# An attention front without queries: transposed x contracted with the context, keys from the squared key weights

## What is computed

```python
# x: (4, 256, 256), ctx: (4, 256, 64)
kv   = ctx @ W_k.T + b_k                                  # (4, 256, 64)
q    = einsum('bij,bjd->bid', layernorm(x), kv)           # the "queries"
sim  = einsum('bid,bjd->bij', q, kv) * 256 ** -0.5
sim  = (sim - mean(sim)) * rsqrt(var(sim) + 1e-6) * gamma + beta
x    = x + tanh(g_xattn) * softmax(sim)
h    = layernorm(x)
score = sigmoid(h @ gate_weight.T)   # 16 experts in 4 groups; best 2 groups, best 4 experts of them
w    = normalised scores of the picked experts * 2.5, zero elsewhere
out  = x + tanh(g_ffn) * (sum_n w[:, n] * swiglu_n(h) + swiglu_shared(h))
```

## Time and profile before

| | |
|---|---|
| median of 3 launches | 205.99 us (205.96 to 206.59) |
| profiled execution, first to last instruction (its span) | 204.2 us |
| PE busy | 186.4 us, 91% |
| DVE busy | 173.8 us, 85% |
| POOL busy | 95.0 us, 46% |
| ACT busy | 83.5 us, 41% |
| moved by DMA | 18.06 MB |

### The profile page before, as it was taken

The page is one execution under the profiler, slowest core; times in us unless marked ns, Lnnn a source line. Parts: engine busy times, 40 slices in busy tenths (PEclk is TensorE's granted clock), DMA queues, the critical chain, the costliest instruction groups (busy, mean ns, idle before and its releaser), DMA issues.

```text
span 204.2 us, 2910 instructions
## 1 busy us (share of the span) xinstructions
PE 186.4 (91%) x809; PEld 142.1 (70%) x809; DVE 173.8 (85%) x332; ACT 83.5 (41%) x164; POOL 95.0 (46%) x101
## 2 busy tenths in 40 slices
PE   7899799859999979897999798999999999999992
PEld 5555578638687657575778566788888888888871
DVE  0859968999899889999889999998988989889853
ACT  2448527323349633333438314233333433434210
POOL 2252352723741746464444534446665466654500
PEclk9999979999999999999999999999999999999998
DMA  6977000003853525250211000321121122221403
GB/s 152 319 226 220 21 0 0 0 0 76 290 159 128 164 98 167 88 171 12 92 62 51 0 3 0 100 62 51 62 78 65 51 51 78 75 53 51 154 0 106
DMA packets 10264, 18.06 MB, mean 88 GB/s; under 512 B 1741, under 2 KB 3789, under 8 KB 10254
## 3 DMA queue, kind: packets, MB, share of 16 engines
q1 hardware_dynamic: 9760, 17.37, 26.7%
...
...
## 4 chain that ended last, share of the span: by engine, by line
PE 48%; DVE 36%; DMA 5%; issue 5%; ACT 3%; DVEq 1%; POOL 0%; SPq 0%; ACTq 0%
PE bank L794 26%; PE bank L838 14%; DVE act_hi L563 5%; DVE act_f L544 4%; DVE act_lo L566 4%; DVE weighted L536 4%; DMA xs<-x_in 3%; DVE logit L495 2%; DVE stats L458 2%; DMA w_row<-weight_rows 2%; PE bank L741 1%; PE bank L724 1%; PE bank L871 1%; DVE ln L470 1%; DVE x L514 1%
## 5 line engine op out<-in xcount | busy, mean ns | idle before, releaser
L279 POOL TENSOR_TENSOR w_lo<-w_raw,w_hi 128x256 fp32r<-128x256 f32 (+1 forms) x72 | 83.6, 1178 | 69.2 <-ACT w_hi L322 68.3
L322 ACT CAST w_hi<-w_raw 128x256 fp32r<-128x256 f32 (+2 forms) x72 | 36.7, 514 | 61.0 <-PE bank L838 36.1
L794 PE MATMUL bank<-hT_hi,w_hi 128*128 128x512 f32 x142 | 56.5, 398 | 0.0
L794 PE MATMUL bank<-hT_lo,w_hi 128*128 128x512 f32 x142 | 56.3, 396 | 0.0
L794 PE MATMUL bank<-hT_hi,w_lo 128*128 128x512 f32 x142 | 44.6, 395 | 0.0
L566 DVE TENSOR_TENSOR act_lo<-act_f,act_hi 128x512 fp32r<-128x512 f32 (+1 forms) x37 | 39.6, 1073 | 1.2
L380 ACT ACTIVATE silu_g<-bank 128x512 f32<-128x512 f32 x36 | 21.6, 600 | 31.9 <-PE bank L794 31.8
L794 PEld LDWEIGHTS bank<-hT_hi,w_lo 128*128 128x128 f32 x142 | 26.7, 188 | 6.4
L794 PEld LDWEIGHTS bank<-hT_hi,w_hi 128*128 128x128 f32 x142 | 26.7, 188 | 6.4
L838 PE MATMUL bank<-act_hi,w_hi 128*128 128x512 f32 (+1 forms) x74 | 23.6, 400 | 8.0 <-DVE act_hi L563 7.9
L794 PEld LDWEIGHTS bank<-hT_lo,w_hi 128*128 128x128 f32 x142 | 26.7, 188 | 6.1
...
## 6 DMA issues: line engine op xcount, KB each, us to landing
...
```

The lines of the kernel that those rows point to most:

```text
L279: nc.gpsimd.tensor_tensor(w_lo[:, par, cols], w_raw[:, bass.ds(n, 1), cols].rearrange("p o c -> p (o c)"), w_hi[:, par, cols].bitcast(F32) ...
L322: nc.scalar.copy(w_hi[:, par, cols], w_raw[:, bass.ds(n, 1), cols].rearrange("p o c -> p (o c)"))\
L794: last = nc.tensor.matmul(dst, w[:, par, w0 + c * P:w0 + (c + 1) * P], m, start=i == 0, stop=i == len(parts) - 1, skip_group_check=True)
```

## The change

The first normalisation of x and the queries go. With c = [ctx, 1] (65 columns) and the key weights with their bias in one array [W_k, b_k] (64 x 65), the similarity of tokens i and j is a product of r_i = sum_j x_ij c_j and u_j = A c_j, where A is the 65 x 65 square of the key weights. PE makes A once (`squared`), u from the context after its mean over the positions was taken out (`offset`, `projected`), and r from x that the host has transposed (`gathered`). A column of A is replaced so that the mean of the row of x drops out (`offset_copy`). Since the keys are centred, a row of similarities has mean zero, and since the second normalisation divides by the row's own spread, the first one's variance is left only in the epsilon: `row_eps` = constant * (var(x) + 1e-5), added to the similarity's variance in place of 1e-6. For batches 0 and 1 gamma is multiplied into the keys (`u_times_gamma`) and PE makes a second similarity with them (`similarity_gamma`), from which `sim_logits` reads; for batches 2 and 3 `sim_scale` takes the place of `sim_centre`.

SP loads transposed x besides x (4 more transfers of 256 KB), in a new order. ACT's queue loads in place of `cw` (276 KB) the key weights (16 KB), transposed context of batch 0 and then of 1 to 3 (65 and 195 KB), and context rows of batch 0 and of 1 to 3 (65 and 195 KB), all ahead of `vec` and `gw`. The statistics of x for batches 2 and 3 move behind `hidden_low(1)`. The gate and up products of steps 0 and 1 are made in two halves by batch (`early_gate`, `early_up`), those of batch 0 ahead of step 0; `route(0)` and `route_back(0)` move into steps 0 and 1. One tile's residual returns from ACT and POOL to DVE.

```diff
+            load_xT(0)
+            load_xT(1)
+            load_x(0)
+            load_x(1)
+            load_slice(0, 0)
+            load_xT(2)
+            load_slice(1, 1)
+            load_xT(3)
+            load_x(2)
+            load_x(3)
             ahead = 8
-            for n in range(ahead):
-                if n >= 2:
-                    sp.wait_ge(w_in[n % 2], 16 * (n // 2))
+            for n in range(2, ahead):
+                sp.wait_ge(w_in[n % 2], 16 * (n // 2))
                 load_slice(n, n % 2)
...
-            for b in range(B):
-                root(0, b)
+            root(1, 0)
+            root(1, 1)
             pool.wait_ge(gwhi_ready, 1)
             nc.gpsimd.tensor_tensor(gw_parts[:, :, E:2 * E], gw[:], gw_parts[:, :, 0:E].bitcast(F32), ALU.subtract)\
               .then_inc(gwlo_ready, 1)
             low_gu(0, 0, 0)
-            root(1, 0)
-            root(1, 1)
-            pool.wait_ge(scaled_ready, 1)
-            nc.gpsimd.tensor_tensor(x1[:, 3, :], prob[:, 3, :], xs[:, 3, :], ALU.add).then_inc(x1_ready[1], 1)
+            low_gu(1, 1, 1)
             root(2, 0)
             root(2, 1)
             pool.wait_ge(hid_ready[1], 2)
             low_d(0, 0, 0)
-            low_gu(1, 1, 1)
             root(1, 2)
...
+            def offset_copy(b):
+                act.wait_ge(offset_done, b + 1)
+                nc.scalar.activation(square[:, b, CD:CA], offset_ps[0:CA, 0:1], ACT.Copy,
+                                     scale=-1.0 / S if b < 2 else 1.0 / S).then_inc(offset_ready, 1)
+
+            def u_copy(b):
+                act.wait_ge(u_done, b + 1)
+                nc.scalar.copy(uT[:, b, :], u_ps[b][0:CA, 0:S]).then_inc(u_ready, 1)
...
-            kv_copy(0)
-            kvT_copy(0)
-            kvT_copy(1)
+            offset_copy(0)
+            u_copy(0)
+            offset_copy(1)
+            u_copy(1)
             act.wait_ge(vec_in, 16)
             nc.scalar.activation(gates[:], vec[:, V_GATES:V_GATES + 2], ACT.Tanh).then_inc(gates_ready, 1)
-            nc.scalar.activation(gamma_scaled[:], gamma, ACT.Copy, scale=SIM_SCALE).then_inc(gamma_ready, 1)
             act.wait_ge(gw_in, 16)
             nc.scalar.copy(gw_parts[:, :, 0:E], gw[:]).then_inc(gwhi_ready, 1)
-            ln_copy(0)
-            ln_copy(1)
-            q_copy(0)
+            act.wait_ge(cT_in, 16)
+            centre_context(2)
+            centre_context(3)
+            for b in (2, 3):
+                offset_copy(b)
+                u_copy(b)
+            softmax_exp(0)
             high_gu(0, 0, 0, 16, False)
-            kv_copy(1)
...
-            softmax_exp(0)
-            kvT_copy(3)
-            ln_copy(2)
-            ln_copy(3)
             softmax_exp(1)
-            q_copy(2)
-            q_copy(3)
-            act.wait_ge(scale_ready[1], 1)
-
-            nc.scalar.activation(prob[:, 3, :], prob[:, 3, :], ACT.Copy, scale=attn_scale[:, 3:4])\
-              .then_inc(scaled_ready, 1)
+            high_gu(1, 1, 1, 16, False)
+            r_copy(2)
+            r_copy(3)
             high_d(0, 0, 0, False)
-            high_gu(1, 1, 1, 16, False)
             hidden_high(0)
...
+            def u_times_gamma(b):
+                dve.wait_ge(u_ready, b + 1)
+                nc.vector.tensor_tensor(uT_gamma[:, b, :], uT[:, b, :], gamma[0:CA, :], ALU.mult)\
+                  .then_inc(u_gamma_ready, 1)
...
+                ts = mean_var(0, b, lambda t: xs[:, t, :])
+                link(nc.vector.tensor_scalar(row_eps[:, ts], meanvar[:, 0, ts, 1], ROW_EPS, ROW_EPS * LN_EPS,
+                                             ALU.mult, ALU.add))
...
             nc.vector.memset(zeros[:].bitcast(F32), 0.0).then_inc(zeros_ready, 1)
+            copy_square()
+            dve.wait_ge(cT0_in, 16)
+            centre_context(0)
+            dve.wait_ge(cT_in, 16)
+            centre_context(1)
+            r_copy(0)
             x_stats(0)
+            r_copy(1)
+            dve.wait_ge(vec_in, 16)
+            u_times_gamma(0)
+            sim_stats(0)
             x_stats(1)
-            normalise(0, 0, 1, xs, ln, ln_ready)
-            normalise(0, 1, 2, xs, ln, ln_ready)
-            x_stats(2)
-            x_stats(3)
...
-            sim_centre(0)
-            sim_logits(0, 5)
+            u_times_gamma(1)
+            sim_logits(0, 1)
             sim_stats(1)
-            sim_centre(1)
-            sim_logits(1, 6)
             dve.wait_ge(gates_ready, 1)
             attention_scale(0)
             residual(0)
+            x1_stats(0)
+            sim_logits(1, 2)
+            normalise(2, 0, 3, x1, hid, hid_ready)
             attention_scale(1)
-            x1_stats(0)
-            residual(1, (2,))
+            residual(1)
             x1_stats(1)
-            normalise(2, 0, 7, x1, hid, hid_ready)
-            normalise(2, 1, 8, x1, hid, hid_ready)
             hidden_low(0)
+            normalise(2, 1, 4, x1, hid, hid_ready)
             hidden_low(1)
+            x_stats(2)
             sim_stats(2)
-            sim_centre(2)
+            sim_scale(2)
+            x_stats(3)
             dve.wait_ge(consts_ready, 2 + 2 * GROUPS - 1)
             add_logits(0)
...
+            def offset(b):
+
+                if b < 2:
+                    pe.wait_ge(sum_dve, b + 1)
+                else:
+                    pe.wait_ge(sum_act, b - 1)
+                if b == 0:
+                    pe.wait_ge(square_ready, 1)
+                else:
+                    pe.wait_ge(offset_ready, b)
+                nc.tensor.matmul(offset_ps[0:CA, 0:1], square[0:CD, B, :], ctx_sum[0:CD, b:b + 1], start=True, stop=True)\
+                  .then_inc(offset_done, 1)
+
+            def projected(b):
+
+                pe.wait_ge(offset_ready, b + 1)
+                if b < 2:
+                    pe.wait_ge(mid_dve, b + 1)
+                else:
+                    pe.wait_ge(mid_act, b - 1)
+                if b == 2:
+                    pe.wait_ge(u_ready, 2)
+                nc.tensor.matmul(u_ps[b][0:CA, 0:S], square[:, b, :], cT_mid[:, b, :], start=True, stop=True)\
+                  .then_inc(u_done, 1)
+
+            def gathered(b):
+
+                pe.wait_ge(xT_in[b], 16)
+                pe.wait_ge(rows0_in if b == 0 else rows_in, 16)
+                if b == 1:
+                    pe.wait_ge(u_ready, 1)
+                if b >= 2:
+                    pe.wait_ge(r_dve, b - 1)
+                for c in range(C):
+                    last = nc.tensor.matmul(r_ps[b][0:CA, 0:S], rows[:, b, c, :], xT[:, b, c, :],
+                                            start=(c == 0), stop=(c == C - 1), skip_group_check=True)
+                last.then_inc(r_done, 1)
...
+            def similarity_gamma(b):
+
+                pe.wait_ge(u_gamma_ready, b + 1)
+                for i in range(2):
+                    last = nc.tensor.matmul(scaled_ps[b][:, i * S:(i + 1) * S], rT[:, b, i * P:(i + 1) * P],
+                                            uT_gamma[:, b, :], start=True, stop=True)
+                last.then_inc(scaled_done, 1)
...
+                if first < 2:
+                    early_gate(first, 1).then_inc(gate_done, 1)
+                    if first == 0:
+                        route(0)
+                    else:
+                        route_back(0)
+                    early_up(first, 1).then_inc(up_done, 1)
+                    return
...
             pe.wait_ge(zeros_ready, 1)
-            keep_warm(10, bank[7])
-            pe.wait_ge(ctxw_in, 16)
-            project(0)
-            project_transposed(0)
-            project_transposed(1)
...
-            for b in (2, 3):
-                transposes(b, lnT_ps, ln, ln_ready, lnT_done)
-            for b in (2, 3):
-                query(b)
-            for b in (2, 3):
-                similarity(b)
-            keep_warm(6, bank[5])
+            pe.wait_ge(r_act, 1)
             hidden(0)
+            early_gate(0, 0)
+            early_up(0, 0)
+            early_gate(1, 0)
+            pe.wait_ge(u_ready, 3)
             hidden(1)
-            first_gate(0)
-            route(0)
+            early_up(1, 0)
             each_step(pe, step, {
```

More of the change, by code:

```diff
@@ L30 @@
 LN_EPS, SIM_EPS = 1e-5, 1e-6
+CA = CD + 1
+ROW_EPS = SIM_EPS / SIM_SCALE ** 2 * S ** 2
 PEN = float(2.0 ** 127)
@@ L87, in build @@
         x1 = sb("x1", [P, NT, D])
-        hid = ln
+        hid = sb("hid", [P, NT, D])
         hT_hi = sb("hT_hi", [P, 2, C, HTOK], F32R)
@@ L94, in build @@
         rstd = sb("rstd", [P, 3, NT])
-        shift = sb("shift", [P, HALF])
+        row_eps = sb("row_eps", [P, NT])
         neg_max = sb("neg_max", [P, NT])
@@ L508, in attention_scale, with residual @@
                   .then_inc(scale_ready[b], 1)
-            def residual(b, ts=None):
+            def residual(b):
                 dve.wait_ge(scale_ready[b], 1)
-                for t in ts or tiles(b):
+                for t in tiles(b):
```

(6 more changed lines are left out.)

250 lines of the change are left out of this document (138 added, 112 removed).

## The result

The changed kernel takes 222.9 us (median of 4 launches, 220.26 to 224.16), the kernel before 206.29 beside it: a ratio of 1.0727 [1.0659, 1.0794]. The ratio leaves out launches over 1.5% above the fastest of their kernel, which can be in a slower state: it rests on 220.26 and 222.07 against 205.96 to 206.59, and by these the change costs 15.0 us, where the medians differ by 16.6. The forecast was 214.6 with a range to 218.0, so the sign was right, and the size, 8.6, little more than half of what came.

The account below looks back on a forecast made before the run. DVE was taken to bound the kernel before 95 us, PE after; the first `act_f` moves the end. Start -3.3, lists +10.0, collision +0.7, PE's clock +1.2 make +8.6 on 206.0: 214.6 us, range 209.5 to 218.0.

Parts of the forecast that it names:

- T: Time at which DVE begins `sim_stats(0)`, the first similarity's statistics: 10.6 us, 3.3 earlier than 13.85, ends 9.6 and 11.7.
- first wait, for the softmax: DVE idle until ACT's first softmax, which stands behind four copies for batches 2 and 3: 2.4 us, new.
- second wait, for POOL's root: DVE idle before `normalise(2, 0)`, as POOL's `root(2, 0)` stands behind `low_gu(1)`: 4.1 us; PE's similarities form another arm.
- third wait, for the second `hT_hi`: DVE idle before `hidden_low(1)`, while PE makes three early blocks and `hidden(1)` and ACT rounds it: 2.3 us.
- T to first `act_f`: Front's stretch from DVE's first similarity statistics to the first `act_f`: 30.7 us by the lists, against 20.7 before.
- first `act_f` to the end: Everything behind the front: length as before, some 170 us, so the end moves as far as the first `act_f`.
- the collision: DVE's `residual(0)` running beside POOL's `low_gu(0)`, a cost beside the lists: 0.7 us, ends 0 and 1.04.
- the front starts late: Rival: transfers in small pieces hold up the front's start, T at 12.5 or more; 216.5 to 219 us, chance 0.1.
- the term for PE's clock: PE idle from about +10 to +14 after T, lowering its clock for work behind: 1.2 us, ends 0 and 2.6.
- DVE alone bounds the front: Rival: DVE's own work sets the front, with an earlier start; `act_f` at 32.5, total 203.9 us, chance 0.08.
- the two side costs don't come: Rival: lists bind, but PE keeps its clock and POOL misses the residual; +6.7, 212.7 us; 211 to 213, chance 0.2.
- the small steps are cheaper: Rival: chain's small steps cheaper than their nearest rows, waits half as long; about 4 less, 208 to 211 us, chance 0.06.

Follow-up runs that it names:

- e12: The changed kernel with eight zero products in place of three at the start, and further ones in PE's gaps of the front: 216.69 us, 1.0495 of the kernel before.
- e5: The changed kernel with ACT's first softmax put ahead of the copies of the offsets and u for batches 2 and 3: 215.55 us, 1.0450 of the kernel before.
- e2 to e6: The changed kernel with lists reordered, as ratios to the kernel before: POOL 1.0815, PE 1.0758, POOL and PE 1.0615, ACT 1.0450, all three 1.0297.
- e1: The changed kernel with eight products of zeros in place of three behind the square of the key weights: 219.57 us, 1.0644 of the kernel before.
- e7: The changed kernel with the POOL, PE and ACT lists reordered and eight products of zeros at the start: 211.32 us, 1.0237 of the kernel before.
- e9: e7 with the context of the first two batches loaded together, earlier on ACT's queue: 211.65 us, 1.0242 of the kernel before.
- e10: e7 with POOL's first root of batch 2 ahead of `low_gu(0)` and DVE's `x_stats` of batches 2 and 3 earlier: 212.93 us, 1.0292 of the kernel before.

## Why the direction was right and the size was not

| | forecast | changed kernel | e12, clock held |
|---|---|---|---|
| T | 10.6 | 14.82 | 12.76 |
| first wait, for the softmax | 2.4 | 5.18 | 3.16 |
| second wait, for POOL's root | 4.1 | 3.66 | 3.66 |
| third wait, for the second `hT_hi` | 2.3 | 4.33 | 2.12 |
| T to first `act_f` | 30.7, and 1.9 beside the lists | 36.87 | 31.45 |
| first `act_f` to the end | 169.6 | 169.9 | 169.0 |

**What was right.** The chain behind T: in e12 it measures 31.45 against 30.7 and the 0.7 for the collision, with all three waits in their places. That the total agrees so closely is partly luck, as the first wait is 0.8 longer than forecast and the other two 0.4 and 0.2 shorter. e5, which has no added zeros, and PE's clock up from 28.83 on, has the second and third at 3.94 and 2.43. e2 to e6 show that the waits are the lists' doing, and that the second comes of two arms which must both be cut. Nothing in the steps takes up the delay: 169.9 against 169.6. The collision of `residual(0)` with `low_gu(0)` cost 1.96 - 0.88 = 1.08, its upper end (0.7 taken).

**What failed, first: the start of the front**, "T = 10.6, 3.3 us earlier" (ends 9.6 and 11.7). It came 4.2 later than that. 2.5 of it is the clock, by e1: I priced every product of the changed start at the 1.13 of the earlier trace rows, a row taken behind ten products of zeros, and never priced the removal of six of them, though the diff of the PE list has it. The rest, 1.7, is landing: the first product with the context's rows starts at 6.95, on their landing, instead of 5.4, and the context of batch 1 landed at 8.2, so that it was centred at about 8.9 instead of 7.4. With the clock up, T follows that landing: 8.36 and 12.33 in e1, 8.79 and 12.76 in e12, 9.23 and 13.20 in e7, 3.97 us each time. The rival "the front starts late" named this cause, at a price of 216.5 to 219; e9 shows that the context's part was worth 1.1 at T once the clock was up. Why these pieces land late (their size, or SP's eight transfers beside them) stays open; no run separates the two. (By the sizes given with the change ACT's queue carries 260 KB more, not the 280 of the prediction's upper end; nothing hangs on it.)

**Second: the term for PE's clock**, 1.2 us with ends 0 and 2.6. It was tied to the one gap of 4 us and to the work behind it. PE was at its low level from T until about 25 (the pair of L823 at 14.96 took 2.08 us, the eight products of L793 at 25.31 only 2.41), through the similarities and the projections that set the first wait, and again from 33.3 to 43.3. From T to `act_f` the changed kernel and e12 differ by 36.87 - 31.45 = 5.4 us: 2.0 up to the first `exp_rec` (10.48 against 8.44), a place for which the sum had no clock term at all, and 3.4 from the first `hid` to the second `hT_lo` (10.25 against 6.86). For that second place the term was also half of what its own rows give: PE's arm there, two similarities of 1.13 and four zeros of 0.25, is 3.3 us at the full clock, so half speed adds 3.3 and not 1.7. From the first similarity to the transposes it measures 2.7 in e12 (28.35 to 31.09), 4.5 in the changed kernel (32.44 to 36.98, where the first pair still took 1.32) and 5.3 in e1 (28.98 to 34.24). So, by e1 and e12, the clock cost 2.5 + 5.4 = 7.9 us where 1.2 stood in the sum. With 1.7 for landing, 0.4 for the collision's upper end, 0.3 less for the lists (31.45 - 1.08 = 30.4 against 30.7) and 0.3 behind `act_f`, that makes 6.7 + 1.7 + 0.4 - 0.3 + 0.3 = 8.8, the whole distance between the forecast of 8.6 and the 17.4 by which the profiled spans differ. It closes because its parts are differences of the same profiles; the launches differ by 15.0 to 16.6, so each part is good to a us or so at best.

The Trainium skill, in TensorE: Matmul & The Clock Gate, section What's actually happening, says that the throttled clock is the default and that activity lifts it. The runs agree: the first four products of zeros of the changed kernel take 2.07 us, 0.52 each, where e12's fourteen at 22.43 take 3.56, 0.25 each; the real products behind the four take nearly twice their time in the earlier trace rows, and with e1's eight zeros in place of the next three they don't.

**The rivals.** "DVE alone bounds the front" was far off. It would have needed the first softmax by +4.2 and the root by +11; they came at +9.3 and +18.6 or so. Even e10, with the waits for both taken away, takes 39.66 - 13.09 = 26.6 us from T to `act_f`, of which DVE waits 1.59 + 1.41 + 2.81 = 5.8 for PE's side; without these, and with the 1.2 of the statistics that it moved out, it would stand at 22.0, where the rival reckoned 21.9. Of the other rivals, "the two side costs don't come" failed on both costs, and "the small steps are cheaper" on the waits, which were not half as long as forecast but 5.18, 3.66 and 4.33. No version tried here beats the kernel before; the best, e7, is 2.4% slower. Holding the clock as e12 does and mending the lists as e7 does were not tried together.
